# A gated graph network with its adjacency loads begun by ScalarE instead of SyncE

## The reference

```python
def _gru_cell(m, h, w_ih, w_hh, b_ih, b_hh):
    gx = m @ w_ih.T + b_ih
    gh = h @ w_hh.T + b_hh
    xr, xz, xn = jnp.split(gx, 3, axis=-1)
    hr, hz, hn = jnp.split(gh, 3, axis=-1)
    r = jax.nn.sigmoid(xr + hr)
    z = jax.nn.sigmoid(xz + hz)
    n = jnp.tanh(xn + r * hn)
    return (1.0 - z) * n + z * h
h = x
for i in range(L):                                # L = 4
    hw = jnp.einsum('bnc,cd->bnd', h, weight[i])
    m = jnp.einsum('bjn,bjd->bnd', adj, hw)
    h = _gru_cell(m, h, w_ih[i], w_hh[i], b_ih[i], b_hh[i])
out = _layernorm(x + h * mask[:, :, None])
```

## Time and profile before

| what | us |
|---|---|
| median of 3 runs (lowest, highest) | 556.23 (554.79, 556.64) |
| the profiled execution's own time | 557.25 |
| its span in the trace | 555.4 |
| DVE busy | 437.7 (79%) |
| ACT busy | 353.2 (64%) |
| POOL busy | 214.6 (39%) |
| PE's mean granted clock, share of full speed | 0.983 |
| DMA, mean over the span | 146 GB/s |

### The profile page before, as it was taken

One profiled execution on the slowest core, in us unless ns is written; L12 is line 12 of the kernel. 1 busy time (PEld: TensorE's weight loads), 2 busy tenths in 40 slices (PEclk: granted clock), 3 DMA queues, 4 the chain that ended last, 5 costly groups with the idle time before them and its releaser, 6 DMA issues.

```text
span 555.4 us, 7447 instructions
## 1 busy us (share of the span) xinstructions
PE 522.8 (94%) x2288; PEld 422.8 (76%) x2288; DVE 437.7 (79%) x737; ACT 353.2 (64%) x568; POOL 214.6 (39%) x161
## 2 busy tenths in 40 slices
PE   5998999999999999999999999999999999999970
PEld 4566888888877888788887888788887788878850
DVE  3997667666988898876888988887788888896666
ACT  3855777647777766756876676755976866354412
POOL 0043333333266333233265532324365633334332
PEclk9998999999999999999999999999999999999985
DMA  7952356345722167365551166435471123223312
GB/s 227 394 196 76 103 187 223 94 133 189 257 104 77 62 214 236 96 187 165 195 210 57 57 208 218 141 115 177 166 280 38 58 76 115 94 76 114 99 35 79
DMA packets 79808, 80.93 MB, mean 146 GB/s; under 512 B 3656, under 2 KB 63648, under 8 KB 79776
## 3 DMA queue, kind: packets, MB, share of 16 engines
q1 hardware_dynamic: 79504, 80.41, 43.6%
q10 hardware_dynamic: 272, 0.13, 0.1%
HBM read 60.08 MB, written 20.45 MB: 145 GB/s over the span
## 4 chain that ended last, share of the span: by engine, by line
DVE 44%; PE 14%; ACT 12%; issue 11%; DMA 11%; POOL 6%; DVEq 1%; SPq 0%; POOLq 0%; ACTq 0%
DMA low<-bounce 9%; DVE y L931 6%; DVE hT_lo L827 5%; PE p_S L472 5%; ACT work L676 5%; DVE work L1120 5%; DVE S_lo L827 4%; DVE work L1126 4%; DVE hT L943 4%; ACT adj_hi L621 3%; DVE work L884 3%; POOL work L1243 3%; DVE nat_lo L827 3%; POOL work L1239 3%; ACT nat_hi L621 2%
## 5 line engine op out<-in xcount | busy, mean ns | idle before, releaser
L1239 POOL TENSOR_TENSOR work<-hT,work 128x512 f32<-128x512 f32 x63 | 83.3, 1322 | 286.4 <-ACT work L676 286.4
L472 PE MATMUL p_S<-adj_hi,nat_hi 128*128 128x512 f32 x480 | 187.4, 390 | 0.0
L472 PE MATMUL p_S<-adj_hi,nat_lo 128*128 128x512 f32 x480 | 186.9, 389 | 0.0
L472 PEld LDWEIGHTS p_S<-adj_hi,nat_lo 128*128 128x128 f32 x480 | 90.2, 188 | 18.5
L472 PEld LDWEIGHTS p_S<-adj_hi,nat_hi 128*128 128x128 f32 x480 | 90.1, 188 | 18.5
L1243 POOL TENSOR_TENSOR work<-work 128x512 f32<-128x512 f32 x63 | 89.6, 1422 | 4.9
L676 ACT ACTIVATE work<-work,bias 128x512 f32<-128x512 f32 x63 | 45.4, 721 | 68.2 <-DVE work L1126 64.2
L1120 DVE SCALAR_TENSOR_TENSOR work<-p_hn,bias,work 128x512 f32<-128x512 f32 x62 | 46.4, 748 | 43.1 <-ACT work L676 42.9
L884 DVE STREAM_TRANSPOSE work<-hT 128x512 f32<-128x512 f32 x62 | 69.1, 1114 | 2.1
L621 ACT ACTIVATE S_hi<-p_S 128x512 fp32r<-128x512 f32 x64 | 37.8, 591 | 42.1 <-PE p_S L472 36.2
L943 DVE TENSOR_TENSOR hT<-work 128x512 f32<-128x512 f32 x63 | 43.2, 686 | 27.0 <-POOL work L1243 27.0
(11 more groups left out here) (149 smaller groups left out, 925.7 us busy)
## 6 DMA issues: line engine op xcount, KB each, us to landing
adj_in<-in_adj_dram SPq DMA_DIRECT2D x64, 512.0 KB, 6.3
bounce<-work SPq DMA_DIRECT2D x62, 256.0 KB, 2.0
low<-bounce SPq DMA_DIRECT2D x62, 256.0 KB, 2.7
x_in<-in_x_dram SPq DMA_DIRECT2D x8, 512.0 KB, 5.8
y<-in_x_dram SPq DMA_DIRECT2D x8, 512.0 KB, 4.2
out_dram<-y SPq DMA_DIRECT2D x7, 512.0 KB, 4.8
y<-in_L_gnn_w_ih_dram SPq DMA_DIRECT2D x2, 192.0 KB, 3.3
y<-in_L_gnn_w_hh_dram SPq DMA_DIRECT2D x2, 192.0 KB, 3.9
```

What stands on the lines that cost most here:

```text
L472: last = nc.tensor.matmul(p_S[h][:, :], part[:, s, j], adj_hi[:, s, j, half(h)], start=(j == 0 and part is nat_hi), stop=(j == NB - 1 and ...
L1239: nc.gpsimd.tensor_tensor(t_sb[:, h], hT[:, s, half(h)], n_sb[:, h], ALU.subtract).then_inc(d_sub, 1)
```

## The change

SP's `next_adj` and its four calls go. ACT gets a function of the same name, with the same two waits and the same transfer, for one block. In steps 1 to 3 it stands in `fill(n)` one place behind the check of the same block: block 0 in place 1 of step 1, block 1 in place 2, and so on to block 7 in place 0 of step 3. In steps 6 and 7 it stands ahead of the conversion of block j and loads block j - 1; block 7 follows in step 7 behind place 2. SP keeps the bounce, x, y and the stores. Its wait on `x_tr` ahead of the loads of x goes too; the wait on `xnat_lo` beside it stays.

```diff
@@ SyncE @@
-            def next_adj(p, s, first, blocks):
-
-                for j in blocks:
-                    sp.wait_ge(adj_checked, NB * (2 * p + 1 + s) + j + 1)
-                    wait_adj(sp, 2 * p + 1 + s, j, first and s == 0)
-                    sp.dma_start(adj_in[:, j], adj_v[2 * p + 2 + s, j]).then_inc(adj_loaded[j], 16)
-
...
-                    if g in (2, 3):
-                        if not last:
-                            next_adj(p, 0, first, range((g - 2) * HB, (g - 1) * HB))
-                        if g == 3 and not first:
-                            store(p - 1, 0)
+                    if g == 3 and not first:
+                        store(p - 1, 0)
...
-                            sp.wait_ge(x_tr, 4 * p + 2 * s + 2)
                             sp.wait_ge(xnat_lo, 2 * p + s + 1)
                             sp.dma_start(x_in[:, s], x_v[2 * p + 2 + s]).then_inc(x_loaded[s], 16)
-                    elif g == STEPS - 2:
-                        next_adj(p, 1, first, range(0, 2))
-                    elif g == STEPS - 1:
-                        next_adj(p, 1, first, range(2, NB))
@@ ScalarE @@
+            def next_adj(p, s, j, first):
+
+                act.wait_ge(adj_checked, NB * (2 * p + 1 + s) + j + 1)
+                wait_adj(act, 2 * p + 1 + s, j, first and s == 0)
+                act.dma_start(adj_in[:, j], adj_v[2 * p + 2 + s, j]).then_inc(adj_loaded[j], 16)
+
...
                     def fill(n):
                         for j in places[n]:
+                            if g >= STEPS - 2 and j:
+                                next_adj(p, 1, j - 1, first)
                             take_adj(*graph_of, j, first and g == 0)
+                        if not last and 1 <= g <= 3 and 0 <= 4 * (g - 1) + n - 1 < NB:
+                            next_adj(p, 0, 4 * (g - 1) + n - 1, first)
                         if g and checks:
                             check_adj(*checks.pop(0))
...
                         if h == 0:
                             fill(2)
                             if g == STEPS - 1 and not last:
+                                next_adj(p, 1, NB - 1, first)
                                 take_adj(p + 1, 1, 0)
```

## The result

The changed kernel takes 600.66 us (median of 4 runs, 599.16 to 602.80) against 556.16 before: ratio 1.0807, 95% interval 1.0767 to 1.0847. I had forecast 565.0 us with 555.5 to 573.0. The direction was right, the size wrong by a factor of five.

A forecast was written before the change was run, and what follows sets the result against it. The kernel was taken as bound by TensorE's work plus a few holes from late ScalarE or VectorE. Traffic 2.1 us plus ScalarE's breaks 6.6 us made 8.7 us, so 565.0 us on the 556.23 median; range 555.5 to 573.

The forecast's parts named there:

- The bound: Whole kernel: time is TensorE's work, busy 94% of the span, plus a few holes when ScalarE or VectorE is late.
- the removed part: SyncE loses 48 issues of 0.343 us with their waits, and one x_tr wait, all beside idle time: gain 0.
- ScalarE's breaks at step 6: Steps 6 and 7: loads between copies make the period 1.75 us instead of 0.945; 1.8 + 2.4 + 2.4 = 6.6 us.
- S_hi of step 7: Sign to look for in the changed profile: S_hi of step 7 over 2 us late against TensorE.
- Issues beside other instructions are free: Steps 1 to 3: each issue hides behind the instruction dispatched before it, 0 to 0.1 us; at most 3.2 us uncovered.
- Traffic: Steps 1 to 3: loads beside bounces cost 0.35 us on three legs, 1.05 us each in pairs 1 and 2, 2.1 us.
- ways of over 3 us: Sign in the changed profile: bounce ways of over 3 us would show rival B; the forecast had 2.3 to 2.5 us.
- rival B: Bounces wait for whole loads, which now leave from another queue: 19.3 us more, 575.5 us, half effect 569; chance 0.17.
- my upper bound: Traffic in steps 1 to 3: a bounce waits for a whole load, 1.23 us each, 4 x 1.23 = 4.9 us.
- pair 0 swallow all of it: Pair 0, steps 1 to 3: ScalarE's slack of 0.40 us and the missing normalising absorb the traffic cost: 0.

The follow-up runs named there:

- e8: The kernel before, with SyncE's 48 later loads cut to 64 of 1024 columns; 556.12 us, ratio 1.0002.
- e4: The changed kernel with every wait and issue in place, but ScalarE's 48 loads carry only 64 of 1024 columns; 564.03 us, ratio 1.0128.
- e3: The kernel before, with ScalarE waiting in steps 6 and 7 for its own previous copy, issuing nothing; 557.80 us, ratio 1.0016.
- e7: The kernel before, but ScalarE issues the loads of steps 1 to 3, two, four and two, in place 2 only; 561.36 us, ratio 1.0093.
- e6: The kernel before, but in pair 0 SyncE issues the eight loads of steps 2 and 3 directly ahead of bounce legs; 570.49 us, ratio 1.0241.
- e2: The changed kernel, but the loads of steps 6 and 7 are SyncE's again, as before; 578.57 us, ratio 1.0402.
- e9: As e7, but ScalarE issues those loads one at a time in four spots behind longer instructions; 558.69 us, ratio 1.0025.
- e10: As e6, but the eight loads carry 512 of 1024 columns (256 KB); 566.48 us, one run.
- e12: The changed kernel with all 48 loads placed otherwise: e9's spots, and singly in steps 6 and 7, none between two copies; 557.77 us, ratio 1.0020.
- e1: The changed kernel, but the loads of steps 1 to 3 are SyncE's again, as before; 573.69 us, ratio 1.0248.

## Why the prediction was wrong

**The bound and the removed part: right.** SyncE's leaving work gave nothing; e8 bounds the whole gain at under 0.2%. PE's length plus holes is how the loss came too, 13.1 us of length and 29.7 of holes; that the length could grow was not in my sum.

**ScalarE's breaks at step 6: right.** 6.6 us forecast, 5.95 in e4. The period is 1.53 to 1.67 us where I took 1.75; S_hi of step 7 was late as said. e3 adds that the wait alone is nearly free (copies 4.47 us for four, 3.88 before); the issue between wait and copy makes the break.

**Issues beside other instructions are free: right, for single ones.** In steps 1 to 3 of the changed kernel an issue of 0.38 us begins just ahead of the copy before it (62.40 against 62.49), and the check follows at once. ScalarE stands idle ahead of its checks behind an issue for 1.5 us in all, six times. The Trainium skill, page "Perfetto Trace Analysis", section "DVE / Act Engine Instruction", has the sequencer push an instruction into a wait queue and go on decoding, and the trace agrees for these places. e7 shows the end of it, 2.70 us of idle behind a group of issues.

**Traffic: the step that failed.** I priced a bounce that meets a load at 0.35 us, three legs a pair, in pairs 1 and 2 only: 2.1 us. By e4 it is the term that makes some 36 of the 44 us. Three things were wrong in it.
First, the price. I chose the row of a bounce at the tail of a burst (2.4 us), which met only what was left of that burst. The case that the change creates, a bounce issued within about a microsecond behind a fresh load, was in no row of the trace of before. It is 2.2 us in e6. In the changed kernel 18 of the 62 ways out took 3.04 to 7.28 us until SyncE's next issue, against 2.05, so 1.0 to 5.2 us extra, the longest where several loads stand beside them. I had named ways of over 3 us as the sign of rival B. Even my upper bound was too low: 1.23 us is the step from load to load inside a burst, where they overlap. The row that I chose was also a mild one of its kind: in six runs (e2, e6, e7, e9, e10, e12) the first way out of the last pair took 4.5 to 5.3 us, where the kernel before has 2.4.
Second, where. I wrote at steps 6 and 7 that only ScalarE's breaks count. But there ScalarE begins a load every 1.67 us just while both halves are on their way, and a bounce stands behind several. e1 puts 17.6 us there, some 6 of which are the breaks. I also let pair 0 swallow all of it in steps 2 and 3; it lost 5.6 us.
Third, the clock. I had treated a hole as worth its length. In the changed kernel each of the five holes of 3.7 us and more is followed by matmuls at the lower clock, which makes most of the 13.1 us by which PE is busy longer; e1 has one of 3.42 us that is not.

**Rival B was the right mechanism with its reason wrong.** It asked for the second queue, and at 19.3 us its price was too low as well. The Trainium skill's page "DMA: Bandwidth & Descriptors", section "Queues, rings and completion order", has each DMA engine go round between queues a packet at a time, which seemed to back it. e6 shows the same kind of delay inside one queue. But order of issue is not all either. The way out at 285.28 has a load 1.48 us ahead of it (and one 5.7 us ahead), others 0.18, 1.85 and 3.51 us behind, all from the other queue, and took 5.0 us; the one at 217.94, with a load 0.88 us ahead and the next one 3.29 us behind, took 3.27. So loads issued behind a bounce from the other queue seem to lengthen it too; no run separates this. The Trainium skill, same page, section "Issuing engines are not separate DMA queues", says that issuing from several engines only saves issue time. The runs agree as far as they go: e12 moves all loads and gains nothing, 1.0020.

**Left open.** Why the extra time of a bounce is 2.2 us behind 512 KB when a load in a burst adds only 1.23, and why it does not fall in proportion with the size. How much the loads behind a bounce add. Why the first way out of the last pair takes over 4 us in some runs: in e7 it takes 5.15 us, though the last load of the burst has landed 1.9 us after it was issued. When a stall lowers the clock. And what is left of e9 and e12 beside the meeting shown above.

## What to carry to other kernels

A short transfer on the critical chain pays for the bulk loads that are under way beside it: in these runs for those issued shortly ahead of it, in its own queue or the other, and it seems also for those that follow from the other queue. When a bulk load is made earlier, or moved to an engine that never waits for the short transfers, look first for the transfer that it will now be ahead of, and price it by a row with a fresh load ahead, not by the tail of a burst. Where no such row exists, the price is unknown, and the range has to say so. A stall of TensorE can cost more than its length, where the clock falls behind it.

## What the runs showed of the hardware

- A 256 KB way out that lands in 2.0 us took 2.88, 3.52 and 4.27 us until the issue behind its landing when 128, 256 or 512 KB were issued 0.38 us ahead in the same queue; up to 7.28 us with loads of the other queue every 1.67 us. A way back took 7.2 us there.
- ScalarE's 48 loads land after 3.6 us in the median, SyncE's 16 first ones, in bursts, after 7.8. The first of a burst of four took 3.7 before.
- ScalarE's issue is 0.344 us in the median (334 to 411 ns), as on SyncE; three in a row took 2.74 us in one place of e7.
- PE's granted clock is below 0.9 in eight of the 40 slices, where the kernel before has three (the fourth, and the last two). Between 300 and 306 us it is 0.50, with matmuls 0.43 us apart right behind a gap of 3.77 us; between 281 and 295 it is 1.00 with 0.225. Behind a gap of 3.42 us in e1 it stays at full, with 0.23.
